# Scan stage of a two-layer sequence model: per-block programs written out in another order, the step's error term moved off VectorE, bias matmuls of double width

## The chip, the cores and the metric

The kernel runs on one core of a Trainium2 chip. The metric is the device time of one execution in microseconds (us). A core has five instruction queues, each of which runs its instructions strictly in the order in which they are listed: TensorE (PE, with its weight loads shown as PEld), VectorE (DVE), ScalarE (ACT), GpSimd (POOL) and SyncE (SP), which here only issues DMA transfers. Queues meet through semaphores: an instruction raises one when it is done, and another queue waits until it has reached a number.

## The reference, cut to what matters

The input is 4096 tokens of 256 features. There are two layers, each of an attention-like block and a feed-forward block, with a layer norm after every sum. The change touches only the second layer:

```
xz = x @ w_in.T + b_in;  x_ssm, z = split(xz);  z = silu(z)
dt = softplus(x_ssm @ w_dt.T + b_dt)
Bm, Cm = x_ssm @ w_B.T + b_B, x_ssm @ w_C.T + b_C          # 16 states
h = exp(A * dt) * h + dt * Bm * x_ssm;  y = sum(h * Cm)     # scan over time, 256 channels x 16 states
y = (y + D * x_ssm) * z
x = layernorm(y @ w_out.T + b_out + x) * gamma + beta
x = layernorm(x)
h = layernorm(x) * ln_gamma + ln_beta
x = layernorm(x + 0.5 * (silu(h @ w1 + b1) @ w2 + b2))      # w1, w2 dequantized, hidden width 1024
```

softplus is computed as max(v, 0) + log(1 + e) with e = exp(-|v|), and the rounding of 1 + e is put back: with s = fl(1 + e), the log term is lessened by (s - 1) - e.

## The kernel before, in words

The second layer's stage ("scan stage") begins after the first layer has left its results in DRAM. The tokens are cut into NB = 8 blocks of TB = 512; each block has NS = 16 states ("slots") n, and the 256 channels are KD = 2 halves k of 128 partitions. For a block b and a state n:

- GpSimd `into(b, n)`: state tile (three in rotation) = uc * B row, 128x1024; it waits until `product` n - 3 and the `carry` of n - 3 are done.
- ScalarE `decay(b, n)`: exp(A * dt) into the two PSUM banks bank_a, one for each k, after the scan of n - 1 has read them; `spread_C(b, n)`: the C row into the one bank bank_c, after `product` n - 1; `carry(b, n)`: the last column of the state into h0.
- VectorE `scan(b, n, k)`: tensor_tensor_scan on 128x512, twice; `product(b, n)`: state times C, 128x1024, into one of two prod tiles. It waits for `add_up` n - 2.
- TensorE `add_up(b, n)`: eight transposes that sum prod into bank_y0 and bank_y1.
- SyncE: the B row and the C row, each broadcast to 128 partitions, four tiles each in rotation.

Around it runs the work of three other blocks. For the next block: `x_proj`, `d_proj`, `bc_proj`, `z_proj` on TensorE, their evacuations and the softplus on ScalarE, `soft_err` on VectorE (L2074), and `soft_fix`, `soft_sum`, `drive` on GpSimd. For the block before: `gate` (VectorE, after the last `add_up`), `turn_gated`, `out_proj`, `residual`, the three layer norms, `turn_normed`, `up_proj`. For the block before that: `silu_up`, `down_proj`, `second`, the last norm and the store. `d_term(b)` opens bank_y of the new block and so waits until `gate` has read the old one. All projections but the up projection start with a bias matmul (64 rows of ones by a bias row) or take the bias on ScalarE; z, out and down have bias matmuls, one for each chunk of 128 tokens, 256 columns wide (L1590, L1627, L1654).

In every program the order is a double loop over blocks `it` and slots `n`; an operation of another block is put at a slot by a line like `if n == 8 and live(nxt): soft_err(nxt)`. In VectorE's program `residual`, `second` and `stats4` each hold their bn_stats and bn_aggr, listed straight behind what they wait for. The last block has its own tail (`end_...`), in halves of 256 tokens.

## Time and profile before

| | |
|---|---|
| median of 3 runs | 1233.45 us (1230.72 to 1236.61) |
| the profiled execution, its own time | 1235.89 us |
| span of the profiled execution (first to last instruction) | 1234.1 us |
| busy over the whole span: PE, DVE, ACT, POOL | 88%, 80%, 72%, 59% |
| scan stage: first scan to last instruction | 587.66 to 1234.1 us |
| mean granted TensorE clock | 0.949 of full |

The share of busy time is taken over the whole span, in which the scan stage is the second half. Its blocks are told apart by the two `gate` instructions (zgs<-bank_y,zgs, L2030), one pair for each block: 651.86, 725.46, 799.35, 873.27, 945.54, 1017.90, 1091.89 and 1161.85 us. Matmul times in the rows are from start to a modelled end and overlap; what a group of matmuls occupies is read from one start to the next.

### The profile page before, as it was taken

What the parts mean: (1) busy time and instruction counts of PE and PEld (TensorE: products, weight loads), DVE (VectorE), ACT (ScalarE), POOL (GpSimd) and SP (SyncE); (2) the same over time, 40 slices, a digit from 0 to 9 for tenths busy, and PEclk for the clock granted to TensorE, in tenths of its full rate; (3) what the DMA queues carried; (4) which work ended last, traced back from release to release, by engine and by line L of the source; (5) the groups of instructions that cost most, each with busy time, mean ns of one, the idle gap of its engine ahead of it and who ended that gap; (6) DMA issues with size and microseconds to landing.
All of it is one profiled execution on the core that took longest, in us unless ns stands there. A gap on an engine that the chain in (4) does not pass through costs nothing.

```text
span 1234.1 us, 17451 instructions
## 1 busy us (share of the span) xinstructions
PE 1082.6 (88%) x5280; PEld 716.2 (58%) x5280; DVE 987.9 (80%) x1326; ACT 890.5 (72%) x1676; POOL 723.2 (59%) x631
## 2 busy tenths in 40 slices
PE   5999999999869999993767799999899999988797
PEld 4677676767644344442445466566575666656476
DVE  5999998999843675452998899999999999999641
ACT  7778877887544456554866888888989888896723
POOL 2555654565631453343785968878697887868220
PEclk9999999999989999996767899999999999999999
DMA  4544324342413001115384544556666484655001
GB/s 131 143 145 125 108 81 131 107 126 62 129 53 120 1 35 52 52 52 158 120 177 119 133 128 121 150 116 147 154 133 152 120 153 122 143 130 145 29 1 35
DMA packets 93233, 133.85 MB, mean 108 GB/s; under 512 B 8786, under 2 KB 47698, under 8 KB 93140
## 3 DMA queue, kind: packets, MB, share of 16 engines
q1 hardware_dynamic: 93140, 132.73, 40.3%
q8 instruction: 43, 0.70, 0.2%
q14 instruction: 50, 0.41, 0.2%
HBM read 116.45 MB, written 14.16 MB: 106 GB/s over the span
## 4 chain that ended last, share of the span: by engine, by line
PE 32%; DVE 9%; ACT 7%; issue 3%; POOL 1%; DVEq 0%; POOLq 0%; ACTq 0%
PE bank_m L39 8%; PE bank_m L1656 7%; DVE state L2017 6%; PE bank_y L1609 4%; PE bank_m L1629 2%; PE bank_m L1592 2%; DVE prod L2023 2%; ACT bank_a L1783 2%; PE bank_y L1600 1%; PE bank_m L1758 1%; ACT bank_c L1788 1%; ACT nT L1864 1%; PE bank_m L1654 1%; PE bank_m L1627 1%; PE bank_y L39 1%
## 5 line engine op out<-in xcount | busy, mean ns | idle before, releaser
L2017 DVE TENSOR_TENSOR_SCAN state<-bank_a,h,state 128x512 f32<-128x512 f32 x256 | 316.4, 1269 | 33.7 <-ACT bank_a L1783 25.2
L2196 POOL TENSOR_TENSOR state<-uc,Bb 128x1024 f32<-128x1024 f32 x64 | 150.7, 2364 | 49.1 <-DVE prod L2023 19.6
L1609 PE MATMUL bank_y<-ident,prod 128*128 128x128 f32 x1024 | 140.9, 286 | 42.2 <-DVE prod L2023 42.1
L2196 POOL TENSOR_TENSOR state<-s,Bb 128x1024 f32<-128x1024 f32 x64 | 150.6, 2363 | 36.7 <-DVE prod L2023 24.8
L1609 PEld LDWEIGHTS bank_y<-ident,prod 128*128 128x128 f32 x1024 | 122.5, 147 | 85.0 <-DVE prod L2023 63.7
L2023 DVE TENSOR_TENSOR prod<-state,bank_c 128x1024 f32<-128x1024 f32 x128 | 156.3, 1221 | 7.9 <-issue 3.1
L1656 PE MATMUL bank_m<-w,f_h 128*128 128x256 f32 x448 | 111.8, 398 | 0.0
L39 PE MATMUL bank_m<-nT,w 128*128 128x512 f32 x224 | 102.0, 597 | 2.7 <-ACT nT L1864 1.7
L1783 ACT ACTIVATE bank_a<-s,A 128x512 f32<-128x512 f32 x128 | 85.5, 686 | 22.6 <-DVE state L2017 21.9
L1783 ACT ACTIVATE bank_a<-dtc,A 128x512 f32<-128x512 f32 x128 | 85.4, 686 | 15.9 <-DVE state L2017 15.2
L1788 ACT ACTIVATE bank_c<-Cb 128x512 f32<-128x512 f32 x128 | 75.5, 590 | 27.4 <-DVE prod L2023 14.3
L1656 PEld LDWEIGHTS bank_m<-w,f_h 128*128 128x128 f32 x448 | 85.2, 197 | 16.6 <-issue 2.8
L668 DVE TENSOR_TENSOR_SCAN L<-abc,zeros,b_id 128x512 f32<-128x512 f32 x64 | 78.4, 1267 | 7.1 <-DMA abc<-decays 4.2
L1314 DVE TENSOR_SCALAR cS<-cS,slope,shift 128x512 f32<-128x512 f32 x24 | 13.1, 546 | 67.5 <-ACT cS L1226 67.5
L39 PEld LDWEIGHTS bank_m<-nT,w 128*128 128x128 f32 x224 | 40.2, 190 | 45.4 <-issue 36.4
L333 PE MATMUL b_op<-W_out,zs 128*128 128x256 f32 x256 | 63.4, 391 | 0.0
L896 POOL TENSOR_TENSOR rms<-ssn,mhalf 128x1 f32<-128x1 f32 x32 | 17.8, 555 | 64.3 <-DVE ssn L697 61.5
L635 DVE SCALAR_TENSOR_TENSOR b_p<-raw,columns,b_p 128x512 f32<-128x512 f32 x72 | 54.1, 752 | 1.3
L871 POOL TENSOR_TENSOR xd<-xs,L 128x512 f32<-128x512 f32 x32 | 33.9, 1059 | 30.9 <-PE b_new L321 14.4
L39 PE MATMUL c<-h,nets 128*128 128x512 f32 x96 | 46.7, 609 | 3.7 <-ACT h L1207 3.6
L39 PE MATMUL b_p<-uh,W_h 128*128 128x512 f32 x132 | 47.2, 439 | 3.0 <-DVE ul L721 2.1
L333 PEld LDWEIGHTS b_op<-W_out,zs 128*128 128x128 f32 x256 | 46.5, 192 | 5.0
(395 smaller groups left out, 2628.8 us busy)
## 6 DMA issues: line engine op xcount, KB each, us to landing
Bb<-CB_rows SPq DMA_DIRECT2D x128, 256.0 KB, 5.0
Cb<-CB_rows SPq DMA_DIRECT2D x128, 256.0 KB, 4.3
abc<-decays SPq DMA_DIRECT2D x32, 512.0 KB, 4.7
Ebc<-ramps SPq DMA_DIRECT2D x64, 128.0 KB, 3.2
uT<-in_uT SPq DMA_DIRECT2D x8, 512.0 KB, 4.4
u<-in_u SPq DMA_DIRECT2D x8, 512.0 KB, 4.2
x_tokens<-x2s SPq DMA_DIRECT2D x8, 512.0 KB, 2.9
x_rows<-x1T SPq DMA_DIRECT2D x8, 512.0 KB, 2.7
```

The source lines that it names most:

```text
L39: i = e.matmul(out, w, x, start=(n == 0), stop=(n == len(pairs) - 1))
L333: i = e.matmul(b_op[:, 0:DM], zs[b % 2][:, m, ts], W_out[:, m, :], start=(m == 0), stop=(m == MD - 1))
L635: e.scalar_tensor_tensor(to, raw[:, m, t:t + TB], cw[:, m, t:t + 1], acc[:, :], ALU.mult, ALU.add).then_inc(v_conv, 1)
L668: e.tensor_tensor_scan(L[:, hs, :].rearrange("p h t -> p (h t)"), abc[g % 2][:, hs, :].rearrange("p h t -> p (h t)"), b_id[:, :], zeros[:, ...
L871: e.tensor_tensor(heads(xd[:, :]), heads(xs[g % 2][:, :]), L[:, :, CH - 1:CH].to_broadcast([P, NH, HD]), ALU.mult).then_inc(p_xd, 1)
L1609: i = e.matmul(p_y[c // 2][:, at:at + P], prod[n % 2][:, k, c * CH:(c + 1) * CH], ident[:, :], start=False, stop=(n == NS - 1), is_transpo ...
L1656: i = e.matmul(to, f_h[:, k, c * CH:(c + 1) * CH], w2[:, k, :], start=False, stop=(k == KF - 1))
L1783: e.activation(p_a[k][:, :], dtc[b % 2][:, k, :], ACT.Exp, scale=A[:, k, n:n + 1]).then_inc(a_a, 1)
L1788: e.activation(p_c[:, :], Cb[n % 4][:, :], ACT.Copy).then_inc(a_c, 1)
L2017: e.tensor_tensor_scan(s[:, k, :], p_a[k][:, :], s[:, k, :], h0[:, n, k:k + 1], ALU.mult, ALU.add).then_inc(v_s, 1)
L2023: e.tensor_tensor(prod[n % 2][:, :, :], state[(NS * b + n) % 3][:, :, :], both(p_c[:, :]), ALU.mult).then_inc(v_g, 1)
L2196: e.tensor_tensor(state[at % 3][:, :, :], uc[b % 2][:, :, :], both(Bb[n % 4][:, :]), ALU.mult).then_inc(p_b, 1)
```

## The change

It rewrites how the five programs of the scan stage are listed, and three pieces of the computation's shape:

1. The loops over slots are gone. Each program is one loop over blocks whose body names every operation in a fixed order, another one than before. `product(n)` mostly stands behind `scan(n + 1, 0)` in place of straight behind `scan(n, 1)`; `gate` stands behind both scans of state 0; on TensorE `turn_gated`, both `out_proj` and the first `x_proj` stand ahead of `d_term` and `add_up(0)`; `up_proj(7)` stands behind `add_up(15)`. The B and C loads are separate and partly out of the order of n.
2. Finer pieces: `decay` by k; the two halves of the norm activations, of `evac_gated`, `evac_normed` and of `turn_...` by themselves; every bn_stats and bn_aggr by itself, so that others stand between; `silu_up` in four pieces of 1024 columns in place of two of 2048.
3. `soft_err` (one VectorE instruction on 128x1024) becomes `minus_one` (ScalarE, Copy with bias -1) and `soft_add` (GpSimd, vl + va), ahead of `soft_fix`.
4. The bias matmuls of z, out and down are 512 columns wide, one for two chunks.
5. The last norm of a block (`norm6`) and its store move some half a block later; in the tail `silu_up` of block Y = 6 stands between and behind the two `end_gated`, and `norm6(Y)`, `second(Y)` and their statistics are interleaved with the tail's own steps.

```diff
+                def load_B(b, n):
+                    if n == 0:
+                        e.wait_ge(st_CB, DMAS * (b + 1))
                     after(e, p_b, NS * b + n - 3)
...
+                for it in range(NB + 3):
+                    old, post, cur, nxt = it - 3, it - 1, it, it + 1
...
+                        load_B(cur, 6)
+                        load_B(cur, 7)
+                        load_B(cur, 5)
...
             def tensor(e):
+                def add_bias(to, part):
+                    e.matmul(to[:, :].rearrange("p (c f) -> p c f", c=2), ones64[:, :],
+                             bias[:, part * DM:(part + 1) * DM].rearrange("p (o f) -> p o f", o=1).to_broadcast([64, 2, DM]), start=True, stop=False)
...
+                    add_bias(pair[p], 1)
                     for c in (0, 1):
-                        e.matmul(to, ones64[:, :], bias[:, DM:2 * DM], start=True, stop=False)
...
-                            e.wait_ge(a_fs, 2 * b + 2)
+                            e.wait_ge(a_fs, 4 * b + 4)
...
+                        down_proj(old, 0, 0)
+                        down_proj(old, 0, 1)
+                        x_proj(cur, 1)
+                        down_proj(old, 1, 0)
+                        add_up(post, 2)
+                        d_proj(cur, 0)
+                        add_up(post, 3)
...
+                        add_up(post, 14)
+                        add_up(post, 15)
+                        up_proj(last, 7)
+                        turn_gated(post, 0)
+                        turn_gated(post, 1)
+                        out_proj(post, 0)
...
+                        out_proj(last, 1)
+                        x_proj(cur, 0)
+                        d_term(post)
+                        add_up(post, 0)
...
             def scalar(e):
+                def minus_one(b):
+                    e.wait_ge(a_sp, 3 * b + 2)
+                    e.activation(flat(uc[b % 2]), flat(uc[b % 2]), ACT.Copy, bias=-1.0).then_inc(v_ve, 1)
...
+                def silu_up(b, h):
+                    part = flat(f_h[:, h * KF // 4:(h + 1) * KF // 4, :])
...
+                        evac_up(last, 7)
+                        evac_gated(post, 0)
+                        decay(cur, 2, 0)
+                        evac_gated(post, 1)
+                        decay(cur, 2, 1)
+                        carry(cur, 1)
+                        decay(cur, 3, 0)
+                        silu_up(last, 0)
+                        spread_C(cur, 1)
+                        silu_up(last, 1)
+                        silu_up(last, 2)
+                        silu_z(cur)
+                        silu_up(last, 3)
+                        spread_C(cur, 2)
+                        decay(cur, 3, 1)
...
+                end_gated(0)
+                silu_up(Y, 0)
+                silu_up(Y, 1)
+                end_gated(1)
+                silu_up(Y, 2)
+                silu_up(Y, 3)
...
             def vector(e):
-                def soft_err(b):
-                    e.wait_ge(a_sp, 3 * b + 2)
-                    e.scalar_tensor_tensor(flat(uc[b % 2]), flat(uc[b % 2]), -1.0, flat(va), ALU.add, ALU.subtract).then_inc(v_ve, 1)
...
+                        scan(post, 15, 1)
+                        product(post, 15)
+                        scan(cur, 0, 0)
+                        scan(cur, 0, 1)
+                        gate(post, 0)
+                        gate(post, 1)
+                        scan(cur, 1, 0)
+                        scan(cur, 1, 1)
+                        scan(cur, 2, 0)
+                        product(cur, 0)
+                        stats6(old, 1)
+                        residual(post, 0)
...
+                        product(cur, 1)
+                        residual(post, 1)
+                        scan(cur, 2, 1)
...
+                        scan(cur, 3, 0)
+                        product(cur, 2)
+                        scan(cur, 3, 1)
+                        product(cur, 3)
+                        scan(cur, 4, 0)
+                        scan(cur, 4, 1)
+                        scan(cur, 5, 0)
+                        product(cur, 4)
...
             def pool(e):
+                def soft_add(b):
+                    e.wait_ge(a_sp, 3 * b + 3)
+                    e.sem_inc(step, 1)
+                    e.tensor_tensor(flat(vl), flat(vl), flat(va), ALU.add).then_inc(p_vs, 1)
...
+                        into(cur, 13)
+                        soft_fix(nxt)
+                        into(cur, 14)
+                        soft_sum(nxt)
+                        into(cur, 15)
+                        drive(nxt)
+                        into(nxt, 0)
```

The conditions `if live(...)` between these lines are left out here. TensorE's and ScalarE's loops begin in the middle of a block, so that their iteration names the scanned block `post` where VectorE's names it `cur`.

## Rows read from the trace of the kernel before

**Rows 1.** The page's chain that ended last: shares of the span by engine.

```profile
PE 32%; DVE 9%; ACT 7%; issue 3%; POOL 1%; DVEq 0%; POOLq 0%; ACTq 0%
```

**Rows 2.** Windows, gate to gate: length, busy of each engine (instructions), clock, DMA, GB/s.

```profile
587.66:651.86 64.20, 43.40 (x174) 29.05 (x172) 61.77 (x50) 47.95 (x83) 48.49 (x21) 0.71 0.64 151
651.86:725.46 73.60, 60.02 (x252) 37.89 (x252) 66.03 (x70) 57.55 (x105) 55.91 (x37) 0.88 0.48 128
725.46:799.35 73.89, 69.54 (x320) 47.79 (x320) 69.09 (x79) 61.87 (x109) 58.56 (x41) 0.98 0.48 129
799.35:873.27 73.92, 69.56 (x320) 47.37 (x320) 69.11 (x80) 63.51 (x112) 58.56 (x41) 0.98 0.56 136
873.27:945.54 72.27, 67.91 (x320) 46.16 (x320) 68.99 (x80) 63.81 (x112) 58.57 (x41) 1.00 0.58 138
945.54:1017.90 72.36, 68.10 (x320) 46.15 (x320) 69.06 (x79) 63.79 (x112) 58.48 (x41) 1.00 0.67 140
1017.90:1091.89 73.99, 69.54 (x320) 47.29 (x320) 70.07 (x81) 63.60 (x113) 58.70 (x41) 0.98 0.53 131
1091.89:1161.85 69.96, 57.83 (x280) 41.24 (x280) 65.78 (x78) 54.13 (x98) 45.84 (x35) 0.95 0.44 106
1161.85:1234.10 72.25, 58.20 (x236) 44.78 (x236) 19.99 (x66) 25.20 (x46) 9.84 (x14) 0.92 0.07 22
```

**Rows 3.** Waits of PE in 873.27:945.54: total us, times, longest.

```profile
PE bank_y L1609 <- DVE prod L2023: 2.6, 2, 1.8
PE bank_y L1600 <- DVE zgs L2030: 1.5, 1, 1.5
```

**Rows 4.** Waits of DVE in 873.27:945.54, the same columns.

```profile
DVE state L2017 <- POOL state L2196: 1.1, 2, 0.8
DVE state L2017 <- ACT bank_a L1783: 0.9, 2, 0.6
```

**Rows 5.** Timeline of DVE in the first block: start, us, engine, line, form, times.

```profile
638.77 2.45 DVE L2017 TENSOR_TENSOR_SCAN state<-bank_a,h,state 128x512 f32<-128x512 f32 x2
641.25 1.22 DVE L2023 TENSOR_TENSOR prod<-state,bank_c 128x1024 f32<-128x1024 f32 x1
642.39 2.45 DVE L2017 TENSOR_TENSOR_SCAN state<-bank_a,h,state 128x512 f32<-128x512 f32 x2
```

**Rows 6.** Source lines of DVE: duration ns min/median/max, first and last start.

```profile
L2074 DVE SCALAR_TENSOR_TENSOR s<-s x4: 2002/2510/3036, 621.3 to 1059.6; 128x1024 f32<-128x1024 f32 x4
L2074 DVE SCALAR_TENSOR_TENSOR uc<-uc,s x3: 1974/2001/2012, 695.3 to 987.2; 128x1024 f32<-128x1024 f32 x3
...
L2017 DVE TENSOR_TENSOR_SCAN state<-bank_a,h,state x256: 1249/1274/1287, 587.7 to 1158.1; 128x512 f32<-128x512 f32 x128
```

**Rows 7.** Groups by form in 945.54:1017.90: busy us, mean ns, idle before.

```profile
L2272 POOL TENSOR_TENSOR s<-s,uc 128x1024 f32<-128x1024 f32 x1 | 2.4, 2362 | 1.3 <-ACT s L1826 1.3
...
L1821 ACT ACTIVATE uc<-s 128x1024 f32<-128x1024 f32 x1 | 1.0, 1040 | 0.0
```

**Rows 8.** Timeline of PE, the first two bias matmuls of one out projection.

```profile
878.34 0.38 PE L1627 MATMUL bank_m<-bias,ones 64*128 64x256 f32 x1
...
879.72 0.39 PE L1627 MATMUL bank_m<-bias,ones 64*128 64x256 f32 x1
```

**Rows 9.** Timeline of PE: the same eight down matmuls in two blocks.

```profile
815.71 3.65 PE L1656 MATMUL bank_m<-w,f_h 128*128 128x256 f32 x8
...
889.63 1.99 PE L1656 MATMUL bank_m<-w,f_h 128*128 128x256 f32 x8
```

**Rows 10.** DMA issues of the scan stage: KB each, median us to landing.

```profile
Bb<-CB_rows SPq DMA_DIRECT2D x124, 256.0 KB, 4.9
...
out<-x3b SPq DMA_DIRECT2D x7, 512.0 KB, 3.3
```

**Rows 11.** Timeline of ScalarE in the tail: the silu of block 6.

```profile
1163.43 3.71 ACT L1876 ACTIVATE f_h<-f_h 128x2048 f32<-128x2048 f32 x2
```

**Rows 12.** Timeline of PE in the tail, with the wait before.

```profile
1167.67 0.58 PE L1728 MATMUL bank_c<-bias,ones 64*128 64x256 f32 x1 [3.82 <-ACT gT L1955]
```

More of the change, by code:

```diff
@@ L1777, in scalar, with decay @@
             def scalar(e):
-                def decay(b, n):
-                    if n == 0:
+                def decay(b, n, k):
+                    if n == 0 and k == 0:
                         e.wait_ge(p_vt, b + 1)
-                    for k in range(KD):
-                        after(e, v_s, 2 * (NS * b + n - 1) + k + 1)
-                        e.activation(p_a[k][:, :], dtc[b % 2][:, k, :], ACT.Exp, scale=A[:, k, n:n + 1]).then_inc(a_a, 1)
+                    after(e, v_s, 2 * (NS * b + n - 1) + k + 1)
+                    e.activation(p_a[k][:, :], dtc[b % 2][:, k, :], ACT.Exp, scale=A[:, k, n:n + 1]).then_inc(a_a, 1)
                 def spread_C(b, n):
@@ L2172, in vector @@
+                gate(Z, 0)
+                gate(Z, 1)
                 end_residual(0)
@@ new lines, in end_root6 @@
+                def end_root6(p):
+                    end_root(rs6[:, half[p]], ve6[:, half[p]], 7 + p, p_l6)
+                into(0, 0)
+                into(0, 1)
+                for it in range(NB + 3):
+                    old, post, cur, nxt = it - 3, it - 1, it, it + 1
+                    if 0 < cur < NB:
+                        into(cur, 1)
+                    if live(cur):
+                        into(cur, 2)
+                        into(cur, 3)
+                        into(cur, 4)
+                    if 0 <= post < NB - 1:
+                        shifted(post)
+                        norm3(post)
+                    if live(cur):
+                        into(cur, 5)
+                    if 0 <= old < NB - 2:
+                        norm6(old)
+                    if live(cur):
+                        into(cur, 6)
+                        into(cur, 7)
+                    if 0 <= post < NB - 1:
+                        scaled(post)
+                    if live(cur):
+                        into(cur, 8)
+                    if 0 <= post < NB - 1:
+                        summed(post)
+                    if live(cur):
+                        into(cur, 9)
+                    if 0 <= post < NB - 1:
+                        norm45(post)
+                    if live(cur):
+                        into(cur, 10)
+                    if live(nxt):
+                        soft_add(nxt)
+                    if live(cur):
+                        into(cur, 11)
+                        into(cur, 12)
+                        into(cur, 13)
+                    if live(nxt):
+                        soft_fix(nxt)
+                    if live(cur):
+                        into(cur, 14)
+                    if live(nxt):
+                        soft_sum(nxt)
+                    if live(cur):
+                        into(cur, 15)
+                    if live(nxt):
+                        drive(nxt)
+                        into(nxt, 0)
@@ L2331, in pool @@
                 norm6(Y)
-                for p in (0, 1):
-                    end_root(rs6[:, half[p]], ve6[:, half[p]], 7 + p, p_l6)
+                end_root6(0)
+                end_root6(1)
             with nc.Block() as block:
```

768 lines of the change are left out of this document (483 added, 285 removed).

## The prediction

> **What bounds the kernel now.** I read the chain of waits first: TensorE holds 32% of it, three times any other engine [rows 1]. That is a share of the whole span, so next come windows cut at the `gate` instructions, one for each block. The reader should see three kinds of block in them [rows 2]: a first without work of its neighbours (64.20 us), five full ones (725.46 to 1091.89, 366.43 us together, mean 73.3), and two with part of the work (73.60 and 69.96), then a tail of 72.25. In a full block PE is busy 67.9 to 69.6 us, DVE 69.0 to 70.1, ACT 61.9 to 63.8, POOL 58.5. Two engines are full at once. The waits say the same from the other side: in the fifth window PE waits 4.1 us for VectorE's products and gate [rows 3], and DVE waits 2.0 us, half for GpSimd's states and half for ScalarE's decays [rows 4]. So neither engine alone sets the 72.3 us: each loses a few microseconds to the other, and a block can fall to about 68 us before one of them has no wait left. Only a change that frees both gives much.
>
> Full blocks come in two lengths, 72.3 and 73.9, and the long ones have a mean clock of 0.98 [rows 2]. The same eight down matmuls took 3.65 us in one and 1.99 in the other [rows 9]: 1.2 in place of 2.4 GHz for some 3.5 us, right behind a PE wait.
>
> **The change, part by part.** The profiled execution took 1235.9 us (span 1234.1 and 1.8 around it), 2.4 above the median shown; the sum is made against it.
>
> *soft_err off VectorE.* Seven instructions of 2.00 to 3.04 us [rows 6]; starts of neighbours lie some 0.07 us closer than recorded ends, as everywhere on this engine, so I charge 1.93 in a full block and 2.95 in the first. In their place ScalarE gets a 128x1024 pass of about 1.04 us and GpSimd one of 2.36 [rows 7], once per block. ACT at 63.8 + 1.0, and 0.3 for `silu_up` in four pieces, and POOL at 58.5 + 2.4 stay below 66 us, so both lie beside the two full engines. If that cover goes, they cost 1.3 and 2.4 us per block.
>
> *product behind the next scan.* Now a state takes 3.62 us, from 638.77 to 642.39; the product starts 2.48 us after the first scan, since it waits for the second one's end; two scans without that wait end at 2.45, the second starting 1.18 after the first [rows 5], so the third place could start at about 2.37. I take 0.09 us for each state, 1.4 per block. Together DVE's listing falls from about 70 us (72.27 less its waits) to 66.7.
>
> *Wide bias matmuls.* One bias and the four matmuls behind it take 1.38 us from start to start [rows 8]; at 0.216 us for each 256 columns (1.73 us of pitch for eight, the 1.99 of rows 9 less the overlap of the last one's end) five would be 1.08. The 0.30 over is paid at each change between the 64-row and the 128-row weights. One wide matmul streams the same columns and changes half as often: 6 x 0.29 = 1.7 us per block. Bounds: nothing, if the overhead goes with columns, and 3.7 if a bias matmul's whole start-to-start time (0.31, twelve times) went. I take 1.7. PE's own work goes from 68.2 (72.27 less 4.1) to 66.5.
>
> *The new order.* No row has it, so I walked one full block, every instruction at its start-to-start time above, each started at the later of its queue and its semaphores; t = 0 is the end of `product(15)`. What matters of it:
> - Head of a block. `add_up(15)` ends at 1.0 and `up_proj(7)` fills PE to 2.7; `gate` ends at 3.7, behind two scans. `turn_gated` to 4.6; the second `evac_gated` stands behind `decay(2, 0)`, which waits for `scan(1, 0)`, so `out_proj` starts at 6.2. PE waits 1.0 + 1.6 there. Then out, x projection and `d_term` run 8.8 us in one piece and `add_up(0)` ends at 16. `product(2)` needs it at 17.0: 1 us to spare.
> - ScalarE's table switch and silu (8.5 us of exp-free work) now have three scans, two products and the statistics in front of VectorE; the walk gives DVE 0.5 us of waiting there.
> - Middle. `add_up(2)` stands behind three down pieces and `x_proj(1)` and ends at 25.3, `product(4)` wants it at 24.2: 1.1. `decay(7, 1)` behind `evac_d(1)`: 0.8. `product(8)` for `add_up(6)` 0.8, `second(1)` for `down_proj(3, 1)` 0.7. PE waits 0.7 for `evac_d(0)`, 0.8 for `evac_bc` (now behind `norm5`, `carry(8)` and others), 1.2 for `product(10)`.
> - End. DVE ends `product(15)` at 69, PE the last `add_up` at 71.6 against 1.0 a block before: 70.6 us, PE setting it, with 5 us of wait left on PE and 4 on DVE.
> - SyncE. Loads out of order hold others: `load_B(5)` stands behind `load_B(7)`, which waits for `into(3)`; it lands 4.9 us later [rows 10], and POOL has `into(4)`, `shifted` and `norm3` (7 us) first. `load_B(10)` waits behind the store and `load_B(12)` for about 36.5 and lands at 41.4 for an `into(10)` at 43. `store_out` lands 3.3 us after its issue, at 39.8, and `second(0)` needs x3b at 40.8. Each is hidden, by 1 to 2 us.
>
> The walk cannot see small waits and clock falls; three full blocks of five lost 1.6 us to the clock before [rows 2]. I add 0.6 and take 71.2 for a full block.
>
> *Blocks apart.* First block: 64.2 - 2.95 - 1.3 = 60.0 (-4.2). Second (651.86 on): PE has only 60 us, so DVE sets it: 73.6 less 6.9 of waits, 1.9 and 1.4 is 63.4, and with 5 of waits 68.5 (-5.1); the 6.9 is what its busy and pitch leave over, the least certain figure here. Five full blocks: 366.4 to 356.0 (-10.4). Last (no soft_err in it): -1.4 and 0.3 of waits (-1.7).
>
> *Tail.* `end_gated` stood behind a table load and 3.71 us of silu [rows 11], and PE waited 3.82 us for it and then ran its out matmuls at half clock [rows 12, 2]. Now it stands ahead of the silu, but behind `norm6(5)`, which waits for POOL behind VectorE's four late bn_aggr: 5.9 us after `product(15)` in place of about 6.4. The second half comes behind two silu pieces. The down matmuls of block 6 start at about 15 in place of 17. What follows is PE's own work, so 2 us stay (-2.0). Bounds: 0 and 4.
>
> Sum: 4.2 + 5.1 + 10.4 + 1.7 + 2.0 = 23.4. 1235.9 - 23.4 = 1212.5, and against the median shown (2.4 lower) 1210. I forecast **1211 us**.
>
> **Where a page speaks against it.** The scans took 1249 to 1287 ns all through a stage in which GpSimd was busy four fifths of the time [rows 6, 2]: a GpSimd pass beside a scan costs the scan nothing. The Trainium skill, Perfetto Trace Analysis, section Optimizing Scalar/DVE Operations, warns that VectorE and GpSimd share an SBUF port and that moving work from one to the other might not help. By that rule `soft_add` would hold VectorE 2.4 us a block; the rows of the scans speak against it.
>
> **The rivals.**
> 1. *Orders cancel* (1225 us). PE stays without real gain: the bias overhead goes with the columns (1.7 us per block back) and the unseen waits take another 1.2. Full blocks then are 72.3 +, about as the better ones before, and only the first, second and last block and the tail gain: 12 us, and 1 of clock. For: PE's 68.2 us are near the 72.3. Against: the x4 group's 0.30 us.
> 2. *The head stalls and the clock falls* (slower, 1243 us). PE waits 1.0 and 1.6 us within 4 us at each head; before, a wait of 1.8 was followed by a half clock in three blocks of five [rows 9, 2]. At 1.2 GHz the 10 us of work up to `add_up(0)` take up to 10 more; the product then waits past its 1 us to spare. It decides at 3.9 us more per full block (23.4 over six blocks): some 8 us of PE's work at half clock. At 5.3 us a block it ends at 1243. Against: the wait before was 1.45 followed at once by 1.80 a few microseconds on, the same sum, and cost 1.6.
> 3. *GpSimd's added pass counts.* Each `soft_add` keeps VectorE out for 2.36 us, seven times 16.5: 1228 us.
> 4. *Waits nearly vanish* (1198 us). Full blocks fall to PE's 66.5 and 2 more: 5 x 2.7 lower than forecast.
> 5. *It does nothing:* the gate-to-gate times stay, because some queue my walk took as hidden (the store behind `norm6`, GpSimd at 61 us) sets them: 1233.
>
> **How the numbers follow.** Forecast case 60%, rival 1 14%, rival 2 9%, rival 3 3%, rival 4 9%, rival 5 5%. 0.5% (6 us) is about what a measurement of this kernel can tell from no change. Faster by more (below 1227.3): forecast, 1, 4, that is 83%, less 1 for the edge of rival 1: 0.82. Slower (above 1239.6): 0.09, the rest 0.09. The forecast's own range is 1204 to 1218 (the full blocks 70 to 72.5, the tail 0 to 4). For 8 in 10 it takes in rivals 1 and 4 in part: 1199 to 1228.
>
> **What would show each step.** Gate-to-gate windows of 71 in place of 73.3, and 68.5 and 60 for the second and first; no DVE scalar_tensor_tensor of 128x1024; scans and products 3.53 us apart in the first block; a bias matmul with its eight followers taking 2.45 us; scans still below 1.29 us; PE waits at a head of 1.0 for the gate and 1.6 for ScalarE; down matmuls of the tail some 15 us after the last product. The forecast is wrong if the clock at the heads is at half, if the PE groups with wide bias take 2.7, or if VectorE waits for `add_up` more than 1 us at `product(2)` or `product(4)`.

## The result, and the profile after

The changed kernel takes 1244.34 us (median of five runs, 1239.96 to 1246.01) against 1232.73 for the kernel before: ratio 1.0085, interval 1.0057 to 1.0113. It is slower by 0.85%, where 1211 and faster had been forecast, and it lies outside the range. Its profiled execution took 1239.96 us, with a span of 1236.6. Times are medians of all executions, ratios and their 95% intervals are taken over those in the chip's faster state alone; only one execution below, of the kernel with the product behind the next scan, was in the slower one.

The windows of the changed kernel, from its first scan, then gate to gate, answer to [rows 2]; the columns are the same.

```profile
582.33:650.15 67.82, 44.70 (x182) 29.84 (x182) 59.40 (x50) 47.89 (x84) 46.85 (x21) 0.75 0.55 131
650.15:723.27 73.12, 59.67 (x248) 38.70 (x248) 62.88 (x70) 58.36 (x104) 59.05 (x38) 0.84 0.60 131
723.27:795.91 72.64, 67.75 (x316) 46.74 (x314) 64.41 (x73) 62.87 (x110) 59.16 (x38) 0.98 0.54 134
795.91:873.25 77.34, 70.28 (x316) 48.84 (x314) 65.92 (x80) 64.89 (x114) 62.32 (x42) 0.93 0.55 132
873.25:946.37 73.12, 66.37 (x314) 47.03 (x313) 65.55 (x79) 64.31 (x114) 59.48 (x42) 0.98 0.58 136
946.37:1020.32 73.95, 67.17 (x318) 45.92 (x316) 65.73 (x80) 64.51 (x114) 60.86 (x41) 1.00 0.63 132
1020.32:1101.02 80.70, 71.61 (x316) 49.98 (x314) 66.00 (x79) 64.98 (x114) 62.05 (x42) 0.92 0.52 126
1101.02:1170.51 69.49, 55.87 (x275) 41.62 (x274) 64.31 (x85) 52.27 (x96) 48.03 (x36) 0.90 0.47 111
1170.51:1236.60 66.09, 54.19 (x234) 43.31 (x232) 19.15 (x67) 27.21 (x52) 11.55 (x18) 0.95 0.07 24
```

Read the third column of busy times first: VectorE's work in a full block fell from 69.0 to 70.1 us [rows 2] to 64.4 to 66.0, as the change intends. The lengths did not follow. Two full blocks take 77.3 and 80.7, with the clock at 0.93 and 0.92, and the other three are about as long as before. So in the long blocks VectorE is idle for 11 to 15 us, and the question is what it waits for. The waits for landed transfers in the scan stage (total, times, longest), first of the kernel before, then of the changed one:

```profile
POOL state L2196 <- DMA Bb<-CB_rows: 6.1, 5, 4.2
```

```profile
POOL state L2492 <- DMA Bb<-CB_rows: 37.8, 17, 5.3
ACT bank_c L1874 <- DMA Cb<-CB_rows: 27.8, 14, 4.7
```

66 us of waits for the rows of B and C stand where 6 stood, and the one on C did not exist before. The longest block shows how they arise. SyncE's queue of the changed kernel (start, time of the group, line, form, times):

```profile
1058.02 0.39 SPq L1543 DMA_DIRECT2D out<-x3b  x1
1058.45 1.50 SPq L1533 DMA_DIRECT2D Bb<-CB_rows  x2
1060.00 0.93 SPq L1539 DMA_DIRECT2D Cb<-CB_rows  x2
1060.97 1.15 SPq L1533 DMA_DIRECT2D Bb<-CB_rows  x1
1062.16 13.96 SPq L1539 DMA_DIRECT2D Cb<-CB_rows  x3
```

By the listing these are the store, B12 and B10, C10 and C11, B13, and C9 as the first of the last group. Nothing is issued for 6 us ahead of the store; then six loads of 256 KB and a store go out within 5 us. The other engines' timeline, right behind:

```profile
1066.77 2.37 POOL L2492 TENSOR_TENSOR state<-uc,Bb 128x1024 f32<-128x1024 f32 x1 [1.26 <-DMA Bb<-CB_rows]
...
1072.59 0.60 ACT L1874 ACTIVATE bank_c<-Cb 128x512 f32<-128x512 f32 x1 [4.68 <-DMA Cb<-CB_rows]
...
1073.28 1.22 DVE L2228 TENSOR_TENSOR prod<-state,bank_c 128x1024 f32<-128x1024 f32 x1 [2.78 <-ACT bank_c L1874]
...
1074.87 1.97 PE L1683 MATMUL bank_m<-ident,xn 128*128 128x128 f32 x8 [4.48 <-ACT xn L1941]
...
1076.63 3.59 PE L1657 MATMUL bank_y<-ident,prod 128*128 128x128 f32 x16
...
1086.66 2.36 POOL L2492 TENSOR_TENSOR state<-uc,Bb 128x1024 f32<-128x1024 f32 x1 [3.58 <-DMA Bb<-CB_rows]
```

C9 was issued at 1062.2 and `spread_C(9)` could start at 1072.6, 10.4 us later. ScalarE stood still for 4.68 us, and with it everything behind it in its list: VectorE's product(9) 2.78 us, and through `norm5` TensorE 4.48 us. In the last row `into(14)` waits at 1086.66 for the same reason at the block's end: B14, whose buffer `into(10)` had freed at 1069.1, goes out only at 1076.6, since it is listed behind C14 and C12, which wait for ScalarE's late spreads, and it lands 10 us later in a new bunch.

The wait for C9 is in the shorter blocks too (4.12 us in the one from 873.25). What sets the two long ones apart begins at their heads. The block from 795.91, with GpSimd and then TensorE:

```profile
795.69 4.67 POOL L2492 TENSOR_TENSOR state<-s,Bb 128x1024 f32<-128x1024 f32 x2 [2.25 <-DMA Bb<-CB_rows]
...
800.71 0.79 PE L1608 MATMUL bank_m<-bias,ones 64*128 64x512 f32 x1 [1.94 <-ACT gT L1930]
801.43 3.78 PE L1676 MATMUL bank_m<-w_o,gT 128*128 128x256 f32 x8
...
877.49 1.99 PE L1676 MATMUL bank_m<-w_o,gT 128*128 128x256 f32 x8
```

B1 (listed behind B2) lands late, so state 1 is late, and with it `scan(1, 0)`, `decay(2, 0)` and the second `evac_gated` behind that decay; TensorE waits 1.94 us for it and then runs its out projection at half clock (the last row is the same group in the block from 873.25, behind a wait of 0.96 us). In the other long block TensorE waits 2.48 us and the group takes 3.78 us again; there the profile puts GpSimd's wait to ScalarE's `carry`. From the gate to `add_up(0)` the two long blocks take 15.8 and 16.5 us, the one from 873.25 takes 11.9. The mean clock of their first 15 us is 0.77, and 1.00 there.

### The profile page after: what moved, and what is told of

Its sections match the earlier page's. It is cut to its first block and busy times, and to the rows that moved or that the text cites. A ratio compares the mean times of both kernels' runs of the same rounds, so it can differ in the third digit from the quotient of the medians.

```text
span 1236.6 us, 17438 instructions
## 1 busy us (share of the span) xinstructions
PE 1068.9 (86%) x5234; PEld 714.4 (58%) x5234; DVE 961.0 (78%) x1319; ACT 896.3 (72%) x1697; POOL 739.6 (60%) x638
## 5 line engine op out<-in xcount | busy, mean ns | idle before, releaser
L2222 DVE TENSOR_TENSOR_SCAN state<-bank_a,h,state 128x512 f32<-128x512 f32 x256 | 319.3, 1272 | 57.6 <-POOL state L2492 27.8
L1657 PE MATMUL bank_y<-ident,prod 128*128 128x128 f32 x1024 | 144.4, 292 | 33.4 <-DVE prod L2228 32.9
L1657 PEld LDWEIGHTS bank_y<-ident,prod 128*128 128x128 f32 x1024 | 127.6, 151 | 65.6 <-DVE prod L2228 46.8
L1702 PE MATMUL bank_m<-w,f_h 128*128 128x256 f32 x448 | 104.7, 383 | 0.0
L1869 ACT ACTIVATE bank_a<-dtc,A 128x512 f32<-128x512 f32 x128 | 86.9, 683 | 12.1 <-DVE state L2222 11.7
L871 POOL TENSOR_TENSOR xd<-xs,L 128x512 f32<-128x512 f32 x32 | 33.9, 1060 | 30.5 <-PE b_new L321 14.5
```

What stands on the lines that cost most here:

```text
L871: e.tensor_tensor(heads(xd[:, :]), heads(xs[g % 2][:, :]), L[:, :, CH - 1:CH].to_broadcast([P, NH, HD]), ALU.mult).then_inc(p_xd, 1)
L1657: i = e.matmul(p_y[c // 2][:, at:at + P], prod[n % 2][:, k, c * CH:(c + 1) * CH], ident[:, :], start=False, stop=(n == NS - 1), is_transpo ...
L1702: i = e.matmul(to, f_h[:, k, c * CH:(c + 1) * CH], w2[:, k, :], start=False, stop=(c % 2 == 1 and k == KF - 1))
L1869: e.activation(p_a[k][:, :], dtc[b % 2][:, k, :], ACT.Exp, scale=A[:, k, n:n + 1]).then_inc(a_a, 1)
L2222: e.tensor_tensor_scan(s[:, k, :], p_a[k][:, :], s[:, k, :], h0[:, n, k:k + 1], ALU.mult, ALU.add).then_inc(v_s, 1)
```

## The experiments

Unless said otherwise each starts from the changed kernel. The kernel before, timed beside them, took 1230.8 to 1234.9 us; a difference of two medians that were not timed together can be off by as much, and the ratios, each against the kernel before timed beside it, are the better measure there.

**The loads, all in order.** B(n), C(n) for each state, the other transfers at fixed places, which moves the two stores and the x loads a little as well; the four other lists as changed:

```diff
-                for it in range(NB + 3):   # the listed loads
...
+                for b in range(NB):
+                    for n in range(NS):
+                        if b > 0 or n > 3:
+                            load_B(b, n)
+                            load_C(b, n)
+                        if n == 0 and b > 0:
+                            load_x2(b - 1)
+                        if n == 2 and 1 < b + 1 < NB:
+                            load_xT(b + 1)
+                        if n == 10 and 0 <= b - 3 < NB - 2:
+                            store_out(b - 3)
+                        if n == 13 and b + 1 < NB:
+                            store_CB(b + 1)
+                load_x2(Z)
+                store_out(Y - 1)
```

> The changed kernel with one part undone: SyncE issues B(n) and C(n) again in the order of n, with the small store, the x loads and the output store between them. All four engines keep the changed lists. Theory A (loads out of order hold others back: GpSimd waited 37.8 us in 17 places for B rows and ScalarE 27.8 us in 14 for C rows, against 6.1 and nearly none before): these waits fall under 10 us together, full blocks go from 75.5 to 71 or 72 us, the first block from 67.8 to some 62, and the kernel takes some 1215 to 1222 us. Theory B (the engines' own lists set the pace: out_proj behind evac_gated, turn_normed behind norm5): the DMA waits may go but full blocks stay above 74, 1235 to 1245 us.

Measured: 1202.94 us (1201.07 to 1204.31), ratio 0.9747 (0.9726 to 0.9769), 41.4 us under the changed kernel. Its windows:

```profile
587.16:649.46 62.30, 41.09 (x182) 27.65 (x182) 59.19 (x50) 47.75 (x84) 49.19 (x22) 0.80 0.61 154
649.46:718.71 69.25, 57.92 (x245) 38.45 (x246) 62.80 (x70) 57.95 (x104) 58.97 (x38) 0.83 0.54 140
718.71:787.68 68.97, 66.02 (x316) 45.93 (x315) 64.30 (x72) 62.44 (x110) 59.08 (x38) 1.00 0.55 141
787.68:858.30 70.62, 67.64 (x315) 46.79 (x314) 65.53 (x80) 64.31 (x114) 60.76 (x42) 0.98 0.51 143
858.30:927.30 69.00, 65.88 (x315) 45.72 (x314) 65.52 (x80) 64.22 (x114) 60.75 (x42) 1.00 0.57 144
927.30:997.99 70.69, 67.75 (x315) 46.65 (x314) 65.31 (x80) 64.36 (x114) 61.01 (x42) 0.98 0.56 144
997.99:1066.84 68.85, 65.67 (x315) 45.71 (x314) 65.48 (x80) 64.13 (x114) 60.55 (x42) 1.00 0.61 140
1066.84:1133.40 66.56, 56.02 (x276) 41.41 (x275) 63.91 (x84) 52.02 (x96) 46.61 (x35) 0.92 0.39 108
1133.40:1201.50 68.10, 55.58 (x234) 43.84 (x232) 19.20 (x67) 27.19 (x52) 11.53 (x18) 0.93 0.07 23
```

VectorE's busy times are those of the changed kernel within 1 us, but the full blocks are all 69 to 71 long, and no wait for B or C is left. So the order of SyncE's queue is the whole loss, and the rest of the change works, better than either theory had it. Issue to landing (median, last column), in the changed kernel and in this one:

```profile
Bb<-CB_rows SPq DMA_DIRECT2D x128, 256.0 KB, 5.2
Cb<-CB_rows SPq DMA_DIRECT2D x128, 256.0 KB, 5.9
```

```profile
Bb<-CB_rows SPq DMA_DIRECT2D x128, 256.0 KB, 4.4
Cb<-CB_rows SPq DMA_DIRECT2D x128, 256.0 KB, 3.6
```

**The changed loads in the old lists.** The kernel before, with only its SyncE program replaced by the changed one (the diff's hunk at SyncE, and no other).

> The kernel before with SyncE's program of the changed kernel alone: B and C rows out of the order of n, the output store and the small store of the next block later. Theory A (an inverted load order harms any such kernel by late rows): slower by 10 to 50 us, with waits of GpSimd and ScalarE for B and C rows of 30 us and more. Theory D (the order of loads fits only with the changed lists and there was harmed by something else): within 5 us of 1233.

Measured: 1270.77 us, ratio 1.0306 (1.028 to 1.0333): 38 us lost, close to the 41. GpSimd waited 79.6 us for B and ScalarE 32.3 for C. This queue is bad beside the old lists too. But its cost there is not of the same make: VectorE also waited 18.6 us in 5 places for the landed store, a wait that neither the kernel before nor the changed one has, so this run does not say what the order of the B and C loads alone costs the old lists.

**Where in the order.** Two loads ahead of the store:

```diff
                         load_C(cur, 8)
+                        load_B(cur, 10)
+                        load_C(cur, 9)
                     if 0 <= old < NB - 2:
                         store_out(old)
                     if live(cur):
                         load_B(cur, 12)
-                        load_B(cur, 10)
                         load_C(cur, 10)
                         load_C(cur, 11)
                         load_B(cur, 13)
-                        load_C(cur, 9)
```

> The changed kernel with two loads moved: B(10) and C(9) are issued ahead of the output store and of B(12), C(10), C(11), B(13); all other loads keep the changed order. In the changed kernel's long blocks C(9) was issued some 4 us behind the store in a bunch of six loads and landed 10 us later; product(9) waited up to 3.5 us for it and turn_normed, behind norm5, up to 4.5. Theory A1 (this one group carries most of the 41 us): these two waits go, 3 to 5 us for each full block, the kernel takes 1215 to 1225 us. Theory A2 (every inversion costs its part): 1225 to 1238 us.

Measured: 1226.17 us, ratio 0.9954 (0.9934 to 0.9974): 18 of the 41 us, at the lower edge of theory A2. ScalarE's waits for C fell from 27.8 to 8.1 us; GpSimd's for B fell little (37.8 to 32.8), and TensorE's for the gated halves at the heads not at all (14.5 us in 7, against 12.1). Then the complement, everything in order but this group (B11 too stays ahead of the store):

```diff
+                        for n in (4, 5, 6, 7, 8):
+                            load_B(cur, n)
+                            load_C(cur, n)
...
                     if 0 <= old < NB - 2:
                         store_out(old)
                     if live(cur):
                         load_B(cur, 12)   # and the five behind it, as changed
...
+                        load_C(cur, 12)
+                        load_C(cur, 13)
```

> The changed kernel with its loads of B and C in the order of their states, except for the group behind the store, which stays as changed (store, B12, B10, C10, C11, B13, C9). It is the other half of e5. Theory (the 41 us of the load order lie in two places, some 18 us in the group behind the store and the other 23 in the groups at a block's start and end): 1244 - 23 = about 1221 us, with waits for B and C landings left only at into(10) and spread_C(9). Rival A (the group behind the store costs nothing by itself, since e5 moved only half of it and the rest of the cost was elsewhere): 1205 us, as with all loads in order. Rival B (the places cover for each other, so one of them left is nearly as bad as all): above 1235 us.

Measured: 1221.55 us, ratio 0.9902 (0.9885 to 0.992). The group costs 18.6 us over the fully ordered kernel, which agrees with the 18 that moving two of its loads gave back; the other 22.8 are what is left of the 41. The waits part the same way: ScalarE's for C are still here (23.9 us in 8), GpSimd's for B are gone (3.7 in 2), and TensorE's at the heads are 6.2 us, at most 1.0, as with all loads in order (6.6, at most 1.0).

**The store's part.** The store behind the group of six, its loads as changed:

```diff
-                    if 0 <= old < NB - 2:
-                        store_out(old)
                     if live(cur):
                         load_B(cur, 12)
...
                         load_C(cur, 9)
+                    if 0 <= old < NB - 2:
+                        store_out(old)
```

> The changed kernel with one line moved: the store of the finished block stands behind the six loads that it stood ahead of (B12, B10, C10, C11, B13, C9, themselves left as changed), and nothing else. Theory A (the store's wait for ScalarE is what blocks the six loads and releases them in a bunch): the group's cost of some 18 us goes, about 1226 us, as in e5 which moved two of the loads ahead of it, and as e9 sizes the group. Theory B (the block is the order in the group itself, B12 waiting for a buffer that into(8) has to free while B10 and C9, due first, stand behind it): no gain, 1238 to 1246 us. Rival C (the store now stands so late that the block behind waits for x3b): over 1250 us.

Measured: 1257.01 us, ratio 1.0207 (1.018 to 1.0233): rival C. GpSimd's waits for B stayed (38.0 us in 15), and VectorE got a new one, of the pass that overwrites x3b on the store that reads it:

```profile
DVE x3b L2266 <- DMA out<-x3b: 32.4, 5, 7.6
```

So two runs more, to part the store from its followers. First the same two loads, but behind the store, at the head of the six:

```diff
                         store_out(old)
                     if live(cur):
+                        load_B(cur, 10)
+                        load_C(cur, 9)
                         load_B(cur, 12)
-                        load_B(cur, 10)
...
-                        load_C(cur, 9)
```

> The changed kernel with B(10) and C(9) moved to the head of the group of six behind the store, the store itself left where the change puts it (e5 had the same two ahead of the store: 1226.2). Theory A (the order inside the group is the cost: B12 and its followers stand ahead of the loads due first, and share the bandwidth with them): 1226 us, as e5. Theory B (the store's own wait for ScalarE is the cost, whatever stands first behind it): about 1241 us, little changed. A value between them gives each its share.

Measured: 1234.49 us, ratio 1.0004 (0.9986 to 1.0023). It lies between the theories. By the medians 10 of the 18 us come from the order inside the group and 8 from standing behind the store's own wait; by the ratios (1.0085, 1.0004, 0.9954) it is 10 and 6. The intervals leave some 3 to 4 us of doubt in each part. And the store alone, two states later, all loads in order:

```diff
-                        if n == 10 and 0 <= b - 3 < NB - 2:
+                        if n == 12 and 0 <= b - 3 < NB - 2:
                             store_out(b - 3)
```

> The changed kernel with all loads in order, and the store of the finished block moved from behind the loads of state 10 to behind those of state 12, two states later; nothing else. Theory (the store's place is bounded on both sides, as e12 showed: VectorE's next pass over x3b waits for the landed store, 32.4 us in five blocks there): two states are some 8 us of issue in each of six blocks, of which the slack of e1 hides an unknown part; 1215 to 1245 us, with a wait of VectorE for the landed store. Rival (e12's loss came from its loads, not from the late store): 1203 us as before.

Measured: 1227.43 us, ratio 0.9941 (0.9926 to 0.9956), 24.5 us over the ordered kernel from one moved line (24 by the ratios). The wait that the late store brought above is there again:

```profile
DVE x3b L2231 <- DMA out<-x3b: 30.6, 5, 6.3
```

The store's place is thus held from both sides: issued too early it blocks the loads behind it until ScalarE is done, too late it makes VectorE wait for its landing.

**The wide bias matmuls alone**, in the kernel before:

```diff
+                    add_bias(pair[p], 1)     # one matmul of 512 columns
                     for c in (0, 1):
-                        e.matmul(to, ones64[:, :], bias[:, DM:2 * DM], start=True, stop=False)
```

> The kernel before with one part of the change alone: one bias matmul of 512 columns in place of two of 256, for z, out and down. Theory A: it takes 0.29 us of TensorE per pair, 1.7 us per full block, of which the block gives back at most 1, since VectorE is full too: 1226 to 1232 us against 1233. Theory B (the overhead goes with the columns): a bias with its eight followers takes 2.7 us as before and the time is that of before.

Measured: 1222.18 us, ratio 0.9905 (0.9885 to 0.9925), more than theory A gave. TensorE's timeline at one out projection, bias to bias:

```profile
871.32 0.49 PE L1564 MATMUL bank_m<-bias,ones 64*128 64x512 f32 x1
871.74 1.99 PE L1633 MATMUL bank_m<-w_o,gT 128*128 128x256 f32 x8
873.66 0.50 PE L1564 MATMUL bank_m<-bias,ones 64*128 64x512 f32 x1
```

That is 2.34 us against 2 x 1.38 = 2.76 before [rows 8]. The other side, the ordered kernel with its bias matmuls narrow again (the same edit, the other way round):

> The changed kernel with loads in order and the old bias matmuls of 256 columns, one for each chunk of 128 tokens. If TensorE sets the pace of a full block (69.6 us there), all of the 0.41 us per pair, 2.5 us a block, comes back: 1202.9 plus 16 to 19, about 1220. If other waits take it up, 1205 to 1213.

Measured: 1211.39 us, ratio 0.9826 (0.9799 to 0.9852): 8.5 us over the ordered kernel, the second case: about half of what TensorE has more to do is taken up by other waits.

**The error term alone**, in the kernel before: `soft_err` gone from VectorE, `minus_one` on ScalarE and `soft_add` on GpSimd in its place, and `soft_fix` one slot later:

```diff
-                        if n == 8 and live(nxt):
-                            soft_err(nxt)      # VectorE
+                        if n == 9 and live(nxt):
+                            minus_one(nxt)     # ScalarE
+                        if n == 9 and live(nxt):
+                            soft_add(nxt)      # GpSimd
```

> The kernel before with one part alone: the error term of the softplus as a ScalarE pass and an added GpSimd pass in place of the VectorE instruction; slots 9 and 10. Theory A (VectorE is freed, the added passes are hidden): 1.9 us less VectorE in a block, 3.0 in the first; TensorE stays at 68 us, so 0.5 to 1.5 us for each block: 1222 to 1230 us. Theory C (the added GpSimd pass makes states late or holds VectorE off the port): scans later by up to 2.4 us a block, 1235 to 1248 us.

Measured: 1231.35 us, ratio 0.9987 (0.997 to 1.0004): nothing that can be told, and neither theory. Seven passes of 2.0 to 3.0 us left VectorE, and it now waits for TensorE where it did not:

```profile
DVE prod L2029 <- PE bank_y L1609: 6.8, 6, 2.2
...
DVE zgs L2036 <- PE bank_y L1609: 2.2, 2, 1.3
DVE x3b L2066 <- PE bank_m L1656: 2.0, 5, 0.4
```

In the kernel before these three were 0.3, 0.9 and 0.4 us: 9.4 us more. VectorE's waits for ScalarE's decays, from 600 us on, rose as well, from 9.2 us in 15 to 15.4 in 17. Together that is 15.6 us, about the 14.5 (seven passes) that VectorE gave up. The other side, the ordered kernel with the pass back on VectorE:

```diff
                         product(cur, 8)
+                    if live(cur + 1):
+                        soft_err(cur + 1)
```

> The changed kernel with loads in order and the error term back on VectorE as one instruction behind product(8), without the ScalarE pass and the GpSimd addition. If VectorE sets the pace: 2 us for each of seven blocks and 3 in the first, 1216 to 1219 us. If TensorE does (it is the fuller one of the two): within 5 us of 1203.

Measured: 1213.67 us, ratio 0.9837 (0.9805 to 0.9869), 10.7 us over the ordered kernel, between the two cases. TensorE, whose waits of this kind come to 2.2 us in the ordered kernel, shows:

```profile
PE bank_m L1648 <- ACT xn L1906: 12.8, 6, 2.2
```

**The order alone**: ordered loads, narrow bias, error term back, so that only the listing of the four other engines and its finer pieces is left.

> The changed kernel with its loads in order, the bias matmuls 256 columns wide again and the error term back on VectorE as one pass: what is left of the change is the order and the smaller pieces of the four engines' lists. By the single removals (8.5 us for the wide bias, 10.7 us for the error term, from 1202.9) and if they add up, this runs in 1222 us, 11 us under the kernel before. Rival (the two cover for each other, and with both gone the lists lose their gain): 1233 us or more. Other rival (each removal costs what it gained when applied alone to the kernel before, 10.7 + 1.5 us): 1215 us.

Measured: 1222.74 us, ratio 0.9911 (0.9883 to 0.9939). The removals add up: 19.8 us over the ordered kernel, against 8.5 + 10.7 = 19.2. The lists and their pieces by themselves are worth some 10 us.

**The product behind the next scan, alone**, in the kernel before, with ScalarE's decays issued piece by piece to allow it:

```diff
                         if live(cur):
                             scan(cur, n, 0)
...
+                            if n > 0:
+                                product(cur, n - 1)
...
                             scan(cur, n, 1)
-                            product(cur, n)
...
+                            next_decay(cur, n, 0)     # ScalarE
+                            spread_C(cur, n)
+                            next_decay(cur, n, 1)
```

> The kernel before with the product of a state listed behind the first scan of the next, and ScalarE's decays listed by k with the C spread between them. All else keeps its slot. Theory A (the wait of product for the second scan's end goes): 3.53 in place of 3.62 us for a state where nothing else stands, 1.4 us a block for VectorE, 4 to 8 us in all: 1225 to 1230. Theory B (TensorE gets its products one scan later and waits more at the head of a block): no gain, 1230 to 1240.

Measured: 1274.86 us (1264.17 to 1283.38 in four executions), ratio 1.0302 (1.0226 to 1.0378), some 37 us by the ratio and beyond both theories. VectorE's waits for decays were 25.2 us in 16 before, of which 16.1 stand ahead of the very first scan. Here they come to the following, in the longest of the four executions, where they may be larger than in the others:

```profile
DVE state L2016 <- ACT bank_a L1782: 68.3, 36, 5.6
```

By the lists it is this. `carry(n)` and ScalarE's other work behind it wait for `scan(n, 1)`, and `decay(n + 2, 0)` behind them is needed at `scan(n + 2, 0)`. Between these two scans VectorE had two scans and two products to run, and now has two scans and one product, so that ScalarE's other work has 1.2 us less to hide behind. No run shows this by itself, since the edit also moved the C spread between the two decays. The opposite edit in the ordered kernel, the products of states 4 to 13 straight behind their own scans, ScalarE's list as changed:

```diff
                         scan(cur, 5, 1)
+                        product(cur, 5)
                         scan(cur, 6, 0)
                         scan(cur, 6, 1)
-                        product(cur, 5)
```

> The changed kernel with its loads in order, and the product of states 4 to 13 again straight behind the second scan of its own state, as in the kernel before; nothing else moved. My forecast's step (0.09 us a state for the product put behind the next scan) expects 10 states x 8 blocks x 0.09 = 7 us more, 1210 us. Rival A (the place of the product is worth nothing once ScalarE's list is the new one, or it costs cover as it did in e4): 1203 us or below. Rival B (the new ScalarE list spreads C only late, so the product now waits for it each time, some 0.5 us a state): 1240 us.

Measured: 1285.27 us, ratio 1.0416 (1.0393 to 1.0439), 82 us for 80 products. Rival B, and twice its price: VectorE's products waited 48.2 us in 30 places for bank_c, and 37.1 in 23 more where the profile names nothing. The timeline, with VectorE, ScalarE and VectorE in turn:

```profile
765.26 2.45 DVE L2187 TENSOR_TENSOR_SCAN state<-bank_a,h,state 128x512 f32<-128x512 f32 x2
...
766.58 0.69 ACT L1834 ACTIVATE bank_a<-dtc,A 128x512 f32<-128x512 f32 x1 [2.54 <-DVE state L2187]
...
768.44 0.69 ACT L1834 ACTIVATE bank_a<-dtc,A 128x512 f32<-128x512 f32 x1
769.05 0.59 ACT L1839 ACTIVATE bank_c<-Cb 128x512 f32<-128x512 f32 x1
...
769.73 1.22 DVE L2193 TENSOR_TENSOR prod<-state,bank_c 128x1024 f32<-128x1024 f32 x1 [2.02 <-ACT bank_c L1839]
```

The product needs `spread_C(n)` (769.05), which ScalarE here lists behind both decays of the next state, and those wait for this state's scans (for other states the spread stands behind the first decay alone). With a scan of state n+1 between, that time is used; without it, it is waited.

## Why the prediction was wrong

The times by window, with the changed loads and with the loads in order:

| | before | forecast | changed | loads in order |
|---|---|---|---|---|
| first block | 64.2 | 60.0 | 67.8 | 62.3 |
| second | 73.6 | 68.5 | 73.1 | 69.3 |
| five full | 366.4 | 356.0 | 377.8 | 348.1 |
| last | 70.0 | 68.3 | 69.5 | 66.6 |
| tail | 72.3 | 70.3 | 66.1 | 68.1 |

**The step that failed** is the walk's last item, "SyncE. Loads out of order hold others", with its verdict "Each is hidden, by 1 to 2 us". Two things in it were wrong.
- The landing time. I gave every load the 4.9 us median of [rows 10], the time of loads issued evenly. Behind a blocked instruction they go out together: C9 came 10.4 us after its issue in the block shown. Some 10 of the group's 18 us lie in the order inside it, the rest in standing behind the store's own wait. The store itself was placed well: it went out at 906.35 in a typical block, 35.5 us after product(15), where the walk had 36.5, and that block's `into(10)` started with no wait for B. It is `spread_C(9)` that waited there, 4.12 us.
- The count. I walked B5, B10 and the store, and neither the C loads nor B1 at the head. C9 stands last of the six though `spread_C(9)` is due before `into(12)`, and ScalarE's 27.8 us of waits for C come on top of GpSimd's.

With 1 to 2 us to spare, an error of 5 us in a landing turns every such place into a wait. I had the kind of mechanism in hand and priced it at nothing; none of the rivals had the loads in it either, except as half a sentence of the fifth. What the runs showed in place of "each is hidden": 66 us of waits for B and C rows, and 41.4 us of the kernel's time.

Rival 2 (head stalls, then half clock) gave 1243 us, near the measured time. Half of its mechanism is in the trace: the heads of the two long blocks do fall to half clock behind a wait, one of the signs by which the prediction called itself wrong. But what set it off there is late rows and not the new heads: with the loads in order the same lists wait 0.96 us at that place, two heads of the five full blocks still run eight matmuls mostly at half clock (3.67 and 3.47 us), and the full blocks take 69 to 71 us. And it is 8.5 us of two blocks, where the rival had 5.3 in each of six. That its number fits is luck. The other two signs did not come: bias and followers took 2.34 us, and VectorE never waited over 0.6 us for `add_up` at a product, with either order of the loads. Rival 1 was also summed wrongly: 2.9 us over the forecast's full block is 74.1 us, not "72.3 +", and its 12 us and 1 of clock from 1233 would give 1220, not 1225.

**The rest of the sum was right in direction and somewhat low.** With ordered loads the change gains 29.8 us (1232.7 to 1202.9), where 23.4 were forecast.
- Full blocks: 69.6 in the mean where the walk gave 70.6 and I took 71.2. The first and second block gained 1.9 and 4.3 us, less than the 4.2 and 5.1 forecast. The last and the tail gained 3.4 and 4.2, where 1.7 and 2.0 stood.
- Wide bias: 0.42 us for each pair where I took 0.29, so about 2.5 a block; in time 10.6 us alone and 8.5 in the new lists. It lies between the bounds of the sum; whether the overhead belongs to the change of weights or to each bias matmul is not shown, as the wide form halves both.
- Error term: seven passes, 14.5 us charged; 10.7 with the new lists and 1.4, which is not to be told from nothing, without. The first paragraph of the prediction says why: more than one engine is nearly full, and what VectorE alone gives up comes back as waits, 9.4 us for TensorE and 6.2 for ScalarE in that run.
- The scans' speed: a GpSimd pass more in each block changed nothing in it (min/median/max, ns, to set beside the last of [rows 6]):

```profile
L2222 DVE TENSOR_TENSOR_SCAN state<-bank_a,h,state x256: 1250/1276/1285, 582.3 to 1166.7; 128x512 f32<-128x512 f32 x128
```

  The warning of the Trainium skill (Perfetto Trace Analysis, Optimizing Scalar/DVE Operations) that work moved between the two engines may not help through their shared port found no support in the scans' durations. But these read one operand from a PSUM bank (bank_a), so they say nothing of instructions with both in SBUF.
- Product behind the next scan: its 0.09 us a state was costed as a term of its own. It is none. In the ordered kernel the pitch is 3.48 us where nothing waits, 0.14 under the 3.62 of [rows 5]:

```profile
909.94 1.19 DVE L2193 TENSOR_TENSOR prod<-state,bank_c 128x1024 f32<-128x1024 f32 x1
911.05 2.45 DVE L2187 TENSOR_TENSOR_SCAN state<-bank_a,h,state 128x512 f32<-128x512 f32 x2
913.42 1.20 DVE L2193 TENSOR_TENSOR prod<-state,bank_c 128x1024 f32<-128x1024 f32 x1
```

But the product's place and ScalarE's order of decays and spreads go together: the old lists with the product moved lost some 37 us, the new ones with it moved back lost 82.
- Clock: the long blocks of the changed kernel run at 0.92 and 0.93. In the block shown TensorE waited 4.48 us and its next group of sixteen identity matmuls took 3.59 us, where another sixteen took 1.91. The clock fell behind waits, and with the loads in order the five full blocks run at 0.98 to 1.00; it is a part of what the loads cost and no cause of its own.

**Open:** how the 22.8 us outside the group of six divide between the block's end (B14 behind C14 and C12) and its head (B1 behind B2), of which only the head's 3.9 and 4.6 us in the two long blocks are read off; and how much of the 41 us is the waits themselves and how much the lower clock behind them. The first block is 5.5 us longer with the changed loads; which load does it was not tried. TensorE waited 16.8 us for xT in that block, and 17.1 with the loads in order, so that wait is no part of the difference; whether it costs anything was not tried either.

## What to carry to other kernels

An in-order queue of transfers is a fifth engine: list it by due times, and give a load that stands behind a wait not the median landing of the trace but that of the bunch which the wait lets go. An order written by hand is right only as a whole: pieces of one engine's list moved alone lost 37 to 82 us here, though the whole gained 30. And before pricing a gain on one of two full engines, price what the other gives at the same time: the same edit was worth nothing measurable alone and 10.7 us in company.

## What the runs showed of the hardware

- Six broadcast loads of 256 KB and a store, issued within 5 us, took up to 10.4 us to land, where 3.6 (C) and 4.4 us (B) are the medians with the loads in the order of the states. The medians of the 512 KB loads between them: x<-x_tokens 7.8 and xT<-x_rows 9.3 us in the changed kernel, 5.4 and 4.1 in the ordered one, 6.9 and 5.2 in the kernel before.
- Over a full block the changed kernel moves 126 to 136 GB/s and the ordered one 140 to 144, so the changed kernel's mean rate was not at a limit.
- A bias matmul of 64 rows among matmuls of 128 rows cost more here than its columns. At the prediction's 0.216 us for 256 columns, bias and followers of a pair come to 2.16 us; narrow they took 2.76, or 0.30 over for each of the two, and wide 2.34, or 0.18 over once. So the overhead did not only halve.
